# Routed feed-forward on one core: one tile begun ahead of the plan in place of three, 159 tiles in place of 161, and the plan's waits as 16-bit numbers

## What is computed

```python
topv, topi = jax.lax.top_k(glogits, TOPK)          # TOPK = 4 of E = 32
gw = jax.nn.softmax(topv, axis=-1)
combine = zeros((N, E)).at[arange(N)[:, None], topi].add(gw)
def body(acc, we):
    wu, wd, ce = we                                # W_up[e], W_down[e], combine[:, e]
    ug = h2 @ wu
    u, g = ug[:, :DFF], ug[:, DFF:]
    return acc + ce[:, None] * (silu(g) * u @ wd), None
y2, _ = jax.lax.scan(body, zeros_like(h2), (W_up, W_down, combine.T))
return x + y2.reshape(Bx, Tx, Dx)
```

## Time and profile before

| | |
|---|---|
| Median of 3 runs | 1031.28 us (1029.86 to 1033.35) |
| Span of the profiled execution | 1031.5 us |
| TensorE busy | 898.5 us (87%) |
| VectorE busy | 805.3 us (78%) |
| ScalarE busy | 512.2 us (50%) |
| GpSimd busy | 552.1 us (54%) |
| DMA | 251.95 MB, mean 244 GB/s |

### The profile page before, as it was taken

The page is one execution under the profiler, slowest core; times in us unless marked ns, Lnnn a source line. Parts: engine busy times, 40 slices in busy tenths (PEclk is TensorE's granted clock), DMA queues, the critical chain, the costliest instruction groups (busy, mean ns, idle before and its releaser), DMA issues.

```text
span 1031.5 us, 21542 instructions
## 1 busy us (share of the span) xinstructions
PE 898.5 (87%) x7336; PEld 738.7 (72%) x7336; DVE 805.3 (78%) x1877; ACT 512.2 (50%) x1193; POOL 552.1 (54%) x513
## 2 busy tenths in 40 slices
PE   3859998988899989988871399999999999999986
PEld 1537676776677767766750288888888888888874
DVE  3878799988978898988857177777777777777787
ACT  1224362735437363453752266666666666566631
POOL 2436466877768688696768133333433344333340
PEclk9869999999999999999995599999999999999998
DMA  7235869687696977959875897778678758663599
GB/s 224 57 93 181 268 218 268 224 275 250 232 290 214 295 241 252 293 192 301 289 252 202 325 307 266 264 243 309 224 254 273 265 186 308 223 226 103 179 365 340
DMA packets 127684, 251.95 MB, mean 244 GB/s; under 512 B 18706, under 2 KB 66327, under 8 KB 127002
## 3 DMA queue, kind: packets, MB, share of 16 engines
q1 hardware_dynamic: 83866, 187.59, 55.4%
q0 software_dynamic: 13872, 34.64, 9.2%
q10 hardware_dynamic: 29840, 28.34, 9.0%
HBM read 136.19 MB, written 102.66 MB: 232 GB/s over the span
## 4 chain that ended last, share of the span: by engine, by line
PE 49%; POOL 14%; DMA 11%; DVE 10%; issue 7%; SPq 4%; ACT 3%; ACTq 0%; DVEq 0%; POOLq 0%
PE scores L970 10%; PE gbank L970 10%; POOL lists L672 10%; PE scores L989 5%; PE gbank L989 5%; DMA w_parts<-ring 4%; PE gbank L761 3%; DMA ring<-in_W_up 3%; POOL ring L679 3%; PE gbank L838 3%; DMA rows_in<-lists 3%; DVE ring L1401 2%; PE gbank L944 2%; PE scores L944 2%; PE gbank L979 2%
## 5 line engine op out<-in xcount | busy, mean ns | idle before, releaser
L694 POOL DMA_INDIRECT pick_rows<-rows_out,pair_i x161 | 160.9, 999 | 269.4 <-ACT rows_out L1232 260.7
L679 POOL TENSOR_TENSOR ring<-ring 128x512 fp32r<-128x512 f32 x96 | 122.6, 1291 | 47.0 <-ACT ring L1167 46.5
L970 PE MATMUL scores<-ring,in_part 128*128 x486 | 134.7, 412 | 0.0
L970 PE MATMUL gbank<-ring,in_part 128*128 x480 | 131.8, 409 | 0.0
L672 POOL DMA_INDIRECT lists<-put_rows,slot_i x104 | 103.4, 994 | 47.5 <-issue 28.0
L838 PE MATMUL gbank<-w_o,ring 128*128 128x256 f32 x512 | 123.2, 396 | 6.0 <-ACT ring L1113 6.0
L761 PE MATMUL gbank<-h_t,w_qk 128*128 128x512 f32 x480 | 122.1, 407 | 6.7 <-DVE h_t L1388 5.0
L1401 DVE SCALAR_TENSOR_TENSOR ring<-gbank,b_qk,rope 128x512 f32<-128x512 f32 x160 | 109.9, 745 | 16.6 <-PE gbank L761 16.0
L838 PEld LDWEIGHTS gbank<-w_o,ring 128*128 128x128 f32 x512 | 99.8, 199 | 26.0 <-ACT ring L1113 9.7
L761 PEld LDWEIGHTS gbank<-h_t,w_qk 128*128 128x128 f32 x480 | 89.7, 192 | 31.5 <-issue 8.6
L1167 ACT ACTIVATE ring<-ring 128x512 fp32r<-128x512 f32 x96 | 59.9, 628 | 90.8 <-DMA w_parts<-ring 50.9
(11 more groups left out here) (200 smaller groups left out, 1899.0 us busy)
## 6 DMA issues: line engine op xcount, KB each, us to landing
w_parts<-ring SPq DMA_DIRECT2D x192, 256.0 KB, 3.2
ring<-w_parts SPq DMA_DIRECT2D x32, 1536.0 KB, 7.9
rows_in<-lists ACTq DMA_DIRECT2D x161, 136.0 KB, 3.8
ring<-in_W_up SPq DMA_DIRECT2D x64, 256.0 KB, 4.0
picks<-pick_rows SPq DMA_DIRECT2D x8, 2048.0 KB, 12.8
ring<-in_W_down SPq DMA_DIRECT2D x32, 256.0 KB, 4.2
q_r<-rot SPq DMA_DIRECT2D x16, 512.0 KB, 6.9
q_r<-ring SPq DMA_DIRECT2D x16, 512.0 KB
```

What stands on the lines that cost most here:

```text
L679: e.tensor_tensor(lower, lower.bitcast(F32), upper.bitcast(F32), ALU.subtract).then_inc(s_lower, 1)
L694: e.indirect_dma_start(out=pick_rows, out_offset=bass.IndirectOffsetOnAxis(ap=pair_i[:, i:i + 1], axis=0), in_=rows_out[i % NY][:, :], in_ ...
L970: ins = e.matmul(front[i % FRONTS], in_parts[i % IN_BUFS][x][:, c, :], ring[:, bass.ds(at + y * WE + c * 2 * DFF, 2 * DFF)], start=k == 0, ...
```

## The change

`AHEAD` goes from 3 to 1. By that `NET`, which is PAIRS / 128 + E - 1 + (AHEAD - 1), goes from 128 + 31 + 2 = 161 to 159. Only expert 0's first tile has constants; every other tile, the first of experts 1 and 2 too, comes from the plan. The table `plan_wait` holds 16-bit numbers in place of 32-bit ones.

```diff
+U16 = mybir.dt.uint16
...
-AHEAD = 3
+AHEAD = 1
 NET = PAIRS // P + E - 1 + (AHEAD - 1)
...
-    plan_wait = sb("plan_wait", [1, 2 * P], I32)
+    plan_wait = sb("plan_wait", [1, 2 * P], U16)
```

## The result

The changed kernel takes 1037.03 us (median of 20 runs, 1030.26 to 1040.34), the kernel before 1033.29 us beside it (20 runs, 1029.08 to 1037.07). The ratio is 1.0035, with an interval of 1.002 to 1.0049: slower by some 3.6 us, where the forecast was 3.8 us faster. Of the 9.5 us between the 1027.5 that was forecast and 1037.03, 2.0 are the kernel before itself, whose median was 1031.28 over three runs and is 1033.29 over twenty. The profiled execution of after took 1040.03 us, with a span of 1038.2; it is one of the long ones. So the two profiles differ by 6.7 us, not by 3.6, and I use them for where time went, and the medians for how much.

The account below looks back on a forecast made before the run. TensorE bounds the middle, the drain of SyncE's transfer queue the end. Row loads 0.7, first gap 2.1 and second gap 1.0 sum to 3.8 us faster, 1027.5 us, range 1025.9 to 1030.9.

Parts of the forecast that it names:

- I take nothing: TensorE's plan_wait reads: 592 ns per eight values already lie hidden behind matmuls, so the 16-bit table changes the time by nothing.
- the sign of a failure: TensorE's table reads: the whole prediction is wrong if the 16-bit loads take over 1.4 us.
- Rival 4: TensorE's queue: 16-bit values load one by one, 2.2 us a load, 0.8 showing 19 times, 15 us slower, 1043; chance 0.08.
- Two tiles fewer: Tile loop: two fill tiles go, ending it 5.06 us sooner for TensorE, ScalarE and VectorE; 3.8 us come out.
- rival 1: At the end: VectorE, not the transfer queue, sets the time, so all 5.06 us come out, 1026.2; chance 0.12.
- The end: After the loop: SP's queue drains from an unmoved start, gaining 0.7 us of row loads, 2.1 and 1.0 of idle gaps.
- the gaps: Slow DMA stretches at 998 to 1002 (193 GB/s) and 1012 to 1014 us (182); closing them gains 2.1 and 1.0 us.
- Rivals 2 and 3: At the end: only the first gap closes, 1028.5; or transfers are at their limit, only row loads gained, 1030.6; 0.12 each.
- The picks still start at 969.6: Start of the end: SP's wait count and the stage before don't move, so the first picks issue at 969.60 us.
- my "nothing" for the seam: Between the halves: row loads 1 and 2 queue behind the 0.73 us plan load, costing nothing; 0.8 us if uncovered.
- The order of the tiles: First expert tiles: loads for experts 4 and 5 release two and one tiles sooner; no change, 1 us either way.
- The limit that the forecast set aside: DMA at the end: the skill's about 358 GB/s per core would leave only the row loads to gain; trace disagrees.

Follow-up runs that it names:

- e2: The kernel before (161 tiles, three begun) with only plan_wait made 16 bits wide: 1037.72 us, ratio 1.0036 to before.
- e4: The changed kernel with plan_slot in 16 bits too: 1041.47 us, ratio 1.0073 to before.
- e1: The changed kernel with plan_wait back in 32 bits, each value clamped to at least 1: 1032.42 us, ratio 0.9985 to before.
- e5: e1 with 64 unused bytes behind the array twice, so the tile buffers stand where they stood before the change: 1029.76 us, ratio 0.996 to before.
- e10: The changed kernel, 16-bit table kept, with 64 unused bytes behind twice that put the tile buffers back: 1036.21 us, ratio 1.0019 to before.
- e3: The kernel before with 159 tiles in place of 161, three begun, 32-bit table with clamp: 1029.86 us, ratio 0.9963 to before.
- e9: e3 with 64 unused bytes that put the tile buffers back; too few tiles for some inputs: 1028.26 us, ratio 0.9942 to before.
- e6: The kernel before with 64 unused bytes behind twice, moving the tile buffers, and the clamp: 1036.13 us, ratio 1.002 to before.
- e8: e5 with 153 tiles in place of 159: 1029.58 us, ratio 0.9953 to before.
- e7: The changed kernel with the 16-bit table read in two halves of four values: 1032.28 us, ratio 0.9982 to before.
- e12: e1 with 96 unused bytes behind twice: 1029.79 us, ratio 0.9974 to before.
- e11: e1 with 32 unused bytes behind twice: 1031.59 us, ratio 0.9982 to before.

## Why the prediction was wrong, step by step

**The 16-bit table: the step that failed.** "I take nothing" was argued from 592 ns that hide. A read took 2.03 us, over the 1.4 that I had named as the sign of a failure. Four comparisons put the price of one such table at 3.7 to 6.1 us (e2 3.7, after and e4 3.9, after and e1 5.2, e5 and e10 6.1). Rival 4 had the mechanism and nearly the size of a read (2.2 us). Its time of 1043 failed at the next step: it let 0.8 us show in 19 places, where the profile of after has a gap in 7, 4.6 us in all (nine and 7.0 by the starts). The mistake was to price an operation that no row showed by "half the bytes". The one row on single values, 0.271 us, was the nearer one, and I gave it 0.08.

**A term that the sum left out: the place of the buffers.** `NET` also sets the size of two arrays. The 64 bytes by which the tile buffers moved cost 1.7 to 2.6 us in three pairs with nothing else changed (after and e10, e3 and e9, e1 and e5), each within its error. The two of a pair stand in different groups and are compared by their ratios. The matmul rows show it directly, and on one and the same chip (e2 and e1, e5 and e6): 277 or 278 ns against 282. No rival had it.

**Two tiles fewer.** 20 plan reads in place of 21, the same 148 activations, and an end shorter by 3.2 us in after and 3.6 to 4.7 in the nine others with 159 tiles, around the 3.8 forecast. By the fit the two tiles are worth 6.0 ± 1.4, which holds rival 1's 5.06 and not my 3.8. Where a further 2 us lies isn't shown: e9's profile has only 3.9 in the end, and the start of its picks differs between executions by more than that.

**The end.** Its course came as written, 10 us late. The sixth pick is issued 25.5 us behind the first, at 1005.01 (forecast 994.7 - 969.6 = 25.1), the eighth 37.7 behind it (37.4), VectorE waits 1.63 us for its last pick (1), and the gaps are closed. e8 refutes rival 1 as a mechanism: with six tiles less still, VectorE waits at every round and the gain is under 1 us, so the transfers are the bound once the gaps are filled. Rivals 2 and 3 fall by the same rows: both gaps went, and 391 to 404 GB/s were held. "The picks still start at 969.6" is wrong by 9.95 us. From the issue of the row loads to the first pick it is 406.9 us for 394.5, 12.4 more. By the starts the reads are 7.0 of it, the longer tiles 2.0, the seam 1.8, and late rows 1.5 (2.8 for 1.3); that is 12.3. The lists were ready 2.4 us earlier in this execution, which leaves the 9.95.

**The seam.** The rows came as forecast (the fourth tile's stand at 586.73, 14.05 us behind the loads, for 14.39; the bound was 589.5). TensorE was slower on them, since its clock rose later after the same work (591.45 for 588.42). From the issue of the loads to the fourth tile's first product it is 20.1 us in after and 18.3 before. This length has two levels in the profiles: 17.9 to 18.4 (before, e1, e2, e6, e7, e9, e12) and 19.3 to 20.1 (after, e3, e4, e5, e8, e10, e11). The levels are those of the clock: it rose 5.8 to 6.7 us behind the first matmul of the seam in all profiles of the shorter level, and 10.4 to 11.8 behind it in all of the longer. The longer one stands in one of five kernels with three begun tiles and in six of nine with one. With one profile each that leaves open whether my "nothing" for the seam was right.

**The order of the tiles.** I gave it ± 1 us; the fit says +2.6 ± 2.0. Both pairs agree (e1 and e3: 0.22%, e5 and e9: 0.18%), though each alone is within its error. In after, e1, e5, e11 and e12 a row made a tile about 0.5 to 1.2 us late at about 620 us; in e4 and e10 it was 0.3 or less and in e7 and e8 nothing, so that is five of the nine kernels with one begun tile. In the five with three (before, e2, e3, e6 and e9) none came late there. That, and the seam's longer level, would be part of it; neither was tried by itself.

**The limit that the forecast set aside.** 391 GB/s were held for 27 us in after, and 404 for 34 us in e8. The Trainium skill's figure of about 358 GB/s ("DMA: Bandwidth & Descriptors", Specifications) is half of what a stack of memory gives, for each of two cores; this kernel runs on one core, and its traces go above it.

**A slip without effect.** The prediction set the span of 1031.5 beside the median of 1031.28. In all runs that show both, the time is 1.75 to 1.94 us above the span, so the profiled execution took about 1033.3 us by this estimate. The sum used only a difference, so nothing hangs on it.

**Left open:** why a read of 16-bit values grows by 0.25 us with each value, why an address modulo 128 matters to a matmul, the last 2 us of the two tiles, why the clock rises at one of two times at the seam, and the late rows. A version that is right for any input and beats both kernels is e5, at 0.996 [0.9935, 0.9985].

## What to carry to other kernels

A register read was priced here by its values and their width, not by its bytes: look for the row of one value, and keep each read shorter than the matmuls that cover it. A loop count that also sizes arrays moves every buffer allocated behind them, so compare the duration of one and the same matmul before and after; a few nanoseconds over thousands of them are microseconds. Where a queue of transfers sets the end, time taken off the engines counts only up to the point at which the queue has no gap left.

## What the runs showed of the hardware

- Eight 16-bit values are loaded into TensorE's registers in 2.03 us (after), four in 0.99 (e7), eight 32-bit values in 0.59 (before, e1).
- Tile buffers at an odd multiple of 64 bytes: 2.53 us a tile, 277 to 278 ns a second product where no gap stands (before, e2, e5, e8, e9, e10). At a multiple of 128 bytes, or 32 bytes off either: 2.54 to 2.55 us and 281 to 283 ns (after, e1, e3, e4, e6, e7, e11, e12).
- One core held 391 GB/s for 27 us and 403 for 10 more (after), and 404 for 34 us (e8), while its engines worked.
- Behind some 22 us without a matmul TensorE stood at the 1.2 GHz level (granted clock 0.50): six matmuls took 2.91 us for 1.64 at 2.4 GHz. Over 14 profiles the clock rose either 5.8 to 6.7 or 10.4 to 11.8 us behind the first matmul.
